# GENConv in a four-layer graph network: two float16 parts in four stored passes instead of three bf16 parts per tile, and other layer ends

## The reference

```python
def _genconv(x, src, dst, W1, W2, gamma, beta, t):
    msg = jax.nn.relu(x[src]) + EPS_MSG
    w = _segment_softmax(msg * t, dst, n)
    aggr = jax.ops.segment_sum(msg * w, dst, num_segments=n)
    h = x + aggr
    h = h @ W1                                  # 128 -> 256
    mu = h.mean(axis=0)
    var = h.var(axis=0)
    h = (h - mu) * jax.lax.rsqrt(var + EPS_BN) * gamma + beta
    h = jax.nn.relu(h)
    return h @ W2                               # 256 -> 128
for l in range(3):
    h = jax.nn.relu(_genconv(h, src, dst, W1[l], W2[l], gamma[l], beta[l], t[l]))
```

## Time and profile before

| | us |
|---|---|
| runs of the kernel before, median of 2 (least, greatest) | 2631.39 (2630.99, 2631.8) |
| the profiled execution, its own time | 2630.21 |
| its span, first to last instruction | 2628.5 |
| PE, PEld, DVE, ACT, POOL busy | 2110.8, 1458.5, 1622.6, 878.1, 1362.6 |
| `genconv`, first instruction to the next stage's first (1226.3 to 2006.4) | 780.1 |
| its three layers, first scatter to first scatter | 256.1 and 256.0; the last to its end 255.7 |
| mean granted TensorE clock over the span (share of 2.4 GHz) | 0.796 |

### The profile page before, as it was taken

One profiled execution on the slowest core, in us unless ns is written; L12 is line 12 of the kernel. 1 busy time (PEld: TensorE's weight loads), 2 busy tenths in 40 slices (PEclk: granted clock), 3 DMA queues, 4 the chain that ended last, 5 costly groups with the idle time before them and its releaser, 6 DMA issues. The chain is left out here.

```text
span 2628.5 us, 46839 instructions
## 1 busy us (share of the span) xinstructions
PE 2110.8 (80%) x9373; PEld 1458.5 (55%) x9374; DVE 1622.6 (62%) x5060; ACT 878.1 (33%) x1968; POOL 1362.6 (52%) x1338
## 2 busy tenths in 40 slices
PE   3588687887989999987999699979987566667766
PEld 1266555547888888874555355435545345545554
DVE  7999521125777777755257625752674677777775
ACT  1499411111212222212111311131113466666663
POOL 2300000003777777751777277637871677777771
PEclk9999788887555555557999799989997677777777
DMA  0000100002444444431111011101113222222221
GB/s 10 4 0 0 39 1 0 0 2 87 120 117 119 118 118 118 118 109 31 17 17 17 9 17 17 15 10 17 17 19 110 73 64 65 64 66 64 64 65 37
DMA packets 197087, 128.42 MB, mean 49 GB/s; under 512 B 138144, under 2 KB 179993, under 8 KB 195872
## 3 DMA queue, kind: packets, MB, share of 16 engines
q0 software_dynamic: 40256, 60.21, 10.2%
q1 hardware_dynamic: 151820, 59.71, 8.8%
q10 hardware_dynamic: 4822, 6.56, 0.8%
HBM read 106.83 MB, written 13.34 MB: 46 GB/s over the span
## 5 line engine op out<-in xcount | busy, mean ns | idle before, releaser
L1783 PE MATMUL ps<-adj,extra 125*128 (+2 forms) x3150 | 606.5, 354 | 35.0 <-DVE extra L1589 35.0
L1480 POOL DMA_INDIRECT edge_rows<-pay,small x425 | 511.7, 1204 | 129.2 <-issue 127.7
L1783 PEld LDWEIGHTS ps<-adj,extra 125*128 125x128 bf16 x3150 | 308.8, 98 | 332.1 <-issue 41.5
L1962 POOL DMA_INDIRECT adj<-h_rows,adj x416 | 396.2, 952 | 136.2 <-issue 65.5
L1157 POOL DMA_INDIRECT work<-p_rows,small x416 | 396.0, 952 | 126.8 <-issue 98.1
L2139 PE MATMUL ps<-adj 128*128 128x125 f32 x928 | 207.1, 360 | 164.2 <-DVE work L2040 159.8
L2139 PEld LDWEIGHTS ps<-adj 128*128 128x128 f32 x928 | 170.8, 254 | 258.5 <-issue 159.2
L1324 PE MATMUL ps<-work 128*128 x1024 | 300.3, 448 | 17.1 <-DVE work L1215 15.5
L1335 PE MATMUL ps<-small,work 128*128 128x64 f32 x1024 | 254.2, 403 | 36.2 <-issue 34.6
L1335 PEld LDWEIGHTS ps<-small,work 128*128 128x128 f32 x1024 | 241.9, 326 | 57.2 <-issue 55.3
L1324 PEld LDWEIGHTS ps<-work 128*128 128x128 f32 x1024 | 238.5, 322 | 26.5 <-issue 23.8
(11 more groups left out here) (347 smaller groups left out, 3015.2 us busy)
## 6 DMA issues: line engine op xcount, KB each, us to landing
work<-dst_all SPq DMA_DIRECT2D x256, 64.0 KB
work<-edge_attr SPq DMA_DIRECT2D x256, 64.0 KB
edge_rows<-pay,small POOLq DMA_INDIRECT x425, 2.7
work<-p_rows,small POOLq DMA_INDIRECT x416
adj<-h_rows,adj POOLq DMA_INDIRECT x416
adj<-adj SPq DMA_DIRECT2D x232, 24.0 KB
pay<-edge_pay SPq DMA_DIRECT2D x106, 46.9 KB
work<-x_kept SPq DMA_DIRECT2D x2, 1562.5 KB, 6.6
```

The source lines that it names most:

```text
L1480: eng.indirect_dma_start(edge_rows[:, :], bass.IndirectOffsetOnAxis(ap=place[:, k:k + 1], axis=0), pay[:, k * ROW:(k + 1) * ROW], None).th ...
L1783: ins = eng.matmul(ps[:, j, 0:cw], parts[k][:, i * D:(i + 1) * D], cols, start=first and i == 0, stop=last and i == 2, skip_group_check=True)
L1962: eng.indirect_dma_start(gathered[:, at:at + D], None, h_rows[:, :], bass.IndirectOffsetOnAxis(ap=row3_i[:, c, DST_C:DST_C + 1], axis=0)). ...
```

## The change

- **Parts.** Instead of three bf16 parts of e and of e*msg there are two float16 parts. The high part is rounded by adding and subtracting `GRID`, the low part is the rest times 2048 (`SPLIT`); the sums of the low part are divided by 2048 when they are read. Values are scaled to at most 32768 (`LARGE`).
- **Passes.** The parts are stored for all tiles, and PE runs four passes over A instead of two: high of e, low of e, low of e*msg, high of e*msg, 175 matmuls each, 700 a layer. Six tiles at a pass's end (four in the second pass) and six at the beginning of the last two are taken piece by piece, so that a PSUM bank is complete, or is needed, one after the other. DVE reads each bank behind each pass (four reads a layer).
- **Who makes them.** The exponent moves to ACT (three activations a tile: exponent, exp, low part), DVE has the weighting, the high part and the rest (three operations a tile). The ring `e` has six tiles.
- **Denominators.** Inverted in 7 pieces of 450 columns during the third pass.
- **Bands.** `BAND` 64 to 4 and `REACH` 70 to 11.
- **Layer end.** x is added with the sums; the second half's relu and the read-outs are shared between ACT and DVE in another way; all of h @ W2's first halves come before the second halves; the greatest values, the transposes and the messages follow piece by piece.
- **Order in the code.** The layers are written out one after the other instead of a loop. The scatters stay where they are: 136, 136, 153, behind the all-reduce and the clearing of each layer. DVE now waits for the clearing (`s_acc`) before the layer's first tile instead of in the middle. `GIN_TURNS` is 0.

```diff
-BAND = 64.0
-REACH = 70.0
+BAND = 4.0
+REACH = 11.0
+LARGE = 32768.0
+SPLIT = 2048.0
+GRID = 768.0
+RINGS, APART = 6, 4
+HEAD, TAIL = [0, 0, 6, 6], [6, 4, 6, 6]
+MARKS = [10, 11, 12, 13, 14, 15, 16]
+GIN_TURNS = 0
...
+    def high_of_exp(s):
+        return high_e_last if isinstance(s, int) and s == NT - 1 else high_e[:, column(s)]
+
+    def low_of_exp(s):
+        return low_e_last if isinstance(s, int) and s == NT - 1 else low_e[:, column(s)]
+
+    def low_of_sum(s):
+        return high_of_exp(s)
+
+    def high_of_sum(s):
+        return apart[:, column(s - FROM)] if isinstance(s, int) and s >= FROM else low_of_exp(s)
+
+    def part_of(p, s):
+        return (high_of_exp, low_of_exp, low_of_sum, high_of_sum)[p](s)
```

SP and POOL:

```diff
+            fill(TURNS - GIN_TURNS, 0, NC - TURNS * 2 * SC)
+            eng.wait_ge(s_x, AL * NP)
+            eng.wait_ge(s_sc[0], 16 * ((TURNS - GIN_TURNS) * SC + NC - TURNS * 2 * SC))
+            eng.wait_ge(s_sc[1], 16 * (TURNS - GIN_TURNS) * SC)
...
-            with eng.Fori(0, AL) as l:
+            for l in range(AL):
                 eng.wait_ge(s_spread, l + 1)
-                eng.nop(nofuse=True)
                 eng.partition_all_reduce(top, lim, D, bass.bass_isa.ReduceOp.max).then_inc(s_top, 1)
 
-                eng.wait_ge(s_copied, 1)
-                eng.wait_ge(s_saved, 16)
-                eng.wait_ge(s_fin, l + 1)
+                if l == 0:
+                    eng.wait_ge(s_copied, 1)
+                    eng.wait_ge(s_saved, 16)
+                    eng.wait_ge(s_max, NP)
+                    eng.wait_ge(s_tr, NGR)
+                else:
+                    eng.wait_ge(s_x, l * NP)
                 eng.memset(acc, 0.0).then_inc(s_acc, 1)
                 with eng.Fori(0, EACH) as i:
                     for b in SETS:
-                        scatter(l * EACH + i, b)
-            for q in range(AL * EACH, TURNS):
+                        scatter(i + l * EACH, b)
+            for q in range(AL * EACH, TURNS - GIN_TURNS):
                 for b in SETS:
                     scatter(q, b)
-            scatter(TURNS, 0, NC - TURNS * 2 * SC)
```

DVE, the band count and the tiles:

```diff
-                step(eng.tensor_tensor(spread, top[:, 0:1], top[:, 1:2], ALU.add))
-                step(eng.tensor_scalar(spread, spread, BAND - REACH, 1.0 / BAND, ALU.add, ALU.mult))
...
+                step(eng.scalar_tensor_tensor(spread, top[:, 0:1], BAND - REACH, top[:, 1:2], ALU.add, ALU.add))
+                step(eng.tensor_scalar(spread, spread, 1.0 / BAND, 0.0, ALU.mult, ALU.max))
+                eng.tensor_scalar(ranges[0:1, l * 2:l * 2 + 1], spread[0:1, :], float(1 << 19), 1.0,
+                                  ALU.min, ALU.add).then_inc(s_band, 1)
...
+                    def high(n):
+
+                        q, s = ORDER[n]
+                        eng.wait_ge(s_w, r * TILES + (n + 1))
+                        if n == 0:
+                            eng.wait_ge(s_sum, r * (4 * NP) + 1)
+                        if q == 1 and s < FROM:
+                            eng.wait_ge(s_used, r * FROM + (s + 1))
+                        eng.tensor_scalar(high_of_sum(s) if q else high_of_exp(s), e[n % RINGS], GRID, -GRID,
+                                          ALU.add, ALU.add).then_inc(s_hi, 1)
+
+                    def rest(n):
+
+                        q, s = ORDER[n]
+                        k = n % RINGS
+                        eng.wait_ge(s_hi, r * TILES + (n + 1))
+                        eng.tensor_tensor(e[k], e[k], high_of_sum(s) if q else high_of_exp(s),
+                                          ALU.subtract).then_inc(s_rest, 1)
...
+                    def produce(n, end):
+                        if n + 2 < end:
+                            weighted(n + 2)
+                        rest(n)
+                        if n + 1 < end:
+                            high(n + 1)
```

DVE, the reads between the passes and the denominators:

```diff
+                    def sum_of(p, j):
+                        eng.wait_ge(s_sum, r * (4 * NP) + (p * NP + j + 2))
+                        return ps[:, j, 0:PIECES[j][2]], den[:, PIECES[j][1]:PIECES[j][1] + PIECES[j][2]]
+
+                    def add_to_x(p, j, scale):
+
+                        y, w = sum_of(p, j)
+                        _, c0, cw = PIECES[j]
+                        eng.scalar_tensor_tensor(y, y, scale, w, ALU.mult, ALU.mult).then_inc(s_num, 1)
+                        eng.wait_ge(s_num, r * (2 * NP) + ((p - 2) * NP + j + 1))
+                        if l == 0 and p == 2 and j == 0:
+                            eng.wait_ge(s_copied, 1)
+                        eng.scalar_tensor_tensor(x[:, c0:c0 + cw], y, widest[:, 0:1], x[:, c0:c0 + cw],
+                                                 ALU.mult, ALU.add).then_inc(s_read, 1)
...
+                    eng.wait_ge(s_mask, r * NP + NP)
                     for j, c0, cw in PIECES:
-                        eng.wait_ge(s_sum, r * (2 * NP) + NP + j + 2)
-                        d, ac = den[:, c0:c0 + cw], acc[:, c0:c0 + cw]
-                        eng.tensor_tensor(d, ps[:, j, 0:cw], d, ALU.mult).then_inc(s_num, 1)
-                        eng.wait_ge(s_num, r * NP + j + 2)
...
+                    def accepted(j):
+                        w = den[:, PIECES[j][1]:PIECES[j][1] + PIECES[j][2]]
+                        eng.wait_ge(s_inv, r * NP + (j + 1))
+                        eng.scalar_tensor_tensor(w, w, float(np.exp(REACH) / LARGE), w, ALU.is_le,
+                                                 ALU.mult).then_inc(s_weight, 1)
+
+                    for j, c0, cw in PIECES:
+                        w = den[:, c0:c0 + cw]
+                        eng.reciprocal(w, w).then_inc(s_inv, 1)
+                        if j:
+                            accepted(j - 1)
+                    accepted(NP - 1)
+                    eng.wait_ge(s_weight, r * NP + NP)
+                    for j in range(NP):
+                        add_to_x(2, j, 1.0 / SPLIT)
+                    for j in range(NP):
+                        add_to_x(3, j, 1.0)
+                    eng.memset(later, 1e37).then_inc(s_more, 1)
+                    eng.tensor_scalar(shift_s, shift_s, -BAND, None, ALU.add).then_inc(s_shift, 1)
                 eng.wait_ge(s_w1, l * 32 + 32)
```

ACT, the tiles:

```diff
+                    def exponent(n):
+
+                        if n == 0:
+                            eng.wait_ge(s_lo, r * TILES + 1)
+                        if n >= RINGS:
+                            eng.wait_ge(s_lo, r * TILES + (n - RINGS + 2))
+                        eng.activation(e[n % RINGS], of_node(ORDER[n][1]), ACT.Relu, bias=shift_s[0:P, :],
+                                       scale=minus_t[0:P, l:l + 1]).then_inc(s_y, 1)
+
+                    def exponential(n):
+                        eng.wait_ge(s_y, r * TILES + (n + 1))
+                        eng.activation(e[n % RINGS], e[n % RINGS], ACT.Exp, scale=-1.0).then_inc(s_e, 1)
+
+                    def low(n):
+
+                        q, s = ORDER[n]
+                        eng.wait_ge(s_rest, r * TILES + (n + 1))
+                        if n == 0:
+                            eng.wait_ge(s_sum, r * (4 * NP) + 1)
+                        if n == NT:
+                            eng.wait_ge(s_sum, r * (4 * NP) + NP + 1)
+                        eng.activation(low_of_sum(s) if q else low_of_exp(s), e[n % RINGS], ACT.Copy,
+                                       scale=SPLIT).then_inc(s_lo, 1)
```

PE, the passes:

```diff
+                    def ready(p, s):
+
+                        at = s if p < 2 else s + (NT + APART)
+                        eng.wait_ge(*((s_hi, r * TILES + (at + 1)) if p in (0, 3) else (s_lo, r * TILES + (at + 2))))
+
+                    def product(p, s, j, last):
+                        _, c0, cw = PIECES[j]
+                        first = isinstance(s, int) and s == 0
+                        if first:
+                            eng.wait_ge(s_read, r * (4 * NP) + (p * NP + j + 1))
+                        if isinstance(s, int):
+                            cols = adj[:, s, c0:c0 + cw]
+                        else:
+                            cols = adj[:, bass.ds(s, 1), c0:c0 + cw].rearrange("p o c -> p (o c)")
+                        ins = eng.matmul(ps[:, j, 0:cw], part_of(p, s), cols, start=first, stop=last,
+                                         skip_group_check=True)
...
+                            ins.then_inc(s_sum, 1)
+                        return ins
+
+                    for p in range(4):
+                        by_piece = NT - TAIL[p]
+                        if HEAD[p]:
+                            ready(p, HEAD[p] - 1)
+                            for j in range(NP):
+                                for s in range(HEAD[p]):
+                                    product(p, s, j, False)
+
+                        def tile(s):
+                            ready(p, s)
+                            for j in range(NP):
+                                ins = product(p, s, j, False)
+                            if p == 1:
```

(44 more changed lines are left out.)

465 lines of the change are left out of this document (209 added, 256 removed).

## The result

The change takes **2517.54 us** (median of 2 runs, 2515.03 to 2520.05) against 2631.39: ratio 0.9567, 95% interval 0.9544 to 0.959. The profiled execution took 2520.05 us (span 2518.3); forecast were 2519, and 2507 to 2546 as the range.

What follows compares the result with a forecast made beforehand. PE bounds the kernel before; after the change POOL's scatters set genconv's layers (208.3 us instead of 256.1). Scatters and turnarounds end at 1885.9, the next stage starts at 1895.4 instead of 2006.4: 2630.2 - 111.0 = 2519 us, range 2507 to 2546.

Steps and rivals of the forecast that it cites:

- Products: PE's matmuls in a genconv layer: 700 instead of 1050 at 192.5 ns, 134.8 us, 67.4 less a layer.
- Parts ready in time: ACT (1.11 us a tile) and DVE (1.00) keep up with PE (1.35); 0 stalls, upper end 15 us a pass boundary.
- Layer ends: PE's time in a genconv layer outside the products: 26.9 to 53.9 us, against 53.9 before.
- POOL's path: A layer's 136 scatters (204.8 us) plus all-reduce and clearing: 208.3 us, longer than PE's 162 to 189.
- The stage's end: After genconv's last scatter, ending at 1885.9 us, x is copied back and the next stage begins at 1895.4.
- Clearing at 0: POOL's clearing, now of 16-bit words, could save 0 to 1.4 us a layer; counted as 0.
- Scatters under another load: POOL's time per scatter in genconv: today's mix kept; bounds 8 us less to 41 us more in sum.
- The rival of 1.30 us: Genconv's scatters stretch to 1.30 us each: 2560 us in all, 41 more; chance 0.07.
- rival 4: TensorE's clock falls within genconv's passes: 313 us a layer, 2801 us in all, slower than before; chance 0.03.
- Bands: One band in each genconv layer; rival of two in all three: about 2830 us, chance 0.02.
- PE's slack: PE's idle time in a genconv layer, waiting for POOL's all-reduce behind the scatters: 19 to 46 us.
- rival 2: PE's path longer than POOL's through stalls and layer ends: 2586 us at worst, middle 2545; chance 0.07.

Runs made afterwards that it cites:

- gin17_plain: Changed kernel with 136 scatters moved to the GIN stage, without most of the piece order: genconv stage 566.3 us against 529.9 with it on the same chip.
- gin17: Changed kernel with 136 scatters (17 turns) moved from the genconv layers to the earlier GIN stage: 2788.99 us, 0.9187 of the kernel before; stage 524.9 us.
- gin8: Changed kernel with 64 scatters (8 turns) moved from the genconv layers to the earlier GIN stage: stage 566.6 us, period 185.3 us.
- after_again: The changed kernel itself, unaltered, run again on another chip than the result's: stage 663.8 us, period 210.0 us.
- before_gin17: The kernel before the change with 136 scatters moved to the GIN stage: ratio 0.9981 to the kernel before, stage 771.8 us, period 256.2 us.

## Why the prediction was right, step by step

- **Products:** 134.8 us a layer predicted, 135.6 measured on the result's chip. In the same order of pieces, 137 to 144 on two others and 154 to 172 on the third show that the price of one matmul from the earlier trace rows is a price of an undisturbed loop; where POOL is the bound, the difference costs nothing.
- **Parts ready in time, 0 for stalls between passes:** right on the result's chip, where the windows above are as full as those of the earlier trace rows. `gin17_plain` shows what the order by pieces does for it: without it the third and fourth pass begin with waits, and a layer is 12.8 us longer.
- **Layer ends, 26.9 to 53.9 us:** `gin17` gives 33.0 and 33.4 (last product to next first product), in the lower half. PE's path is then 169 on the result's chip (208.3 between two first products, less 46.22 idle, plus the 6.69 that follow the all-reduce in `gin17`) and 174 to 176 bare on the two other chips; predicted were 162 to 189.
- **POOL's path 208.3 us:** measured 209.9 and 208.9 from first scatter to first scatter. The scatters' first layer took 205.5 us from first to last start instead of 203.6, in part for one of 2002 ns; the turnaround took 3.2 instead of 3.5. `gin8` gives 1.48 us for a scatter taken out, and the sum had 1.506.
- **The stage's end:** the last scatter ended at 1886.5 (1885.9 predicted), SP issued the copy at 1887.96, and the next stage began at 1895.50 (1895.4). That these agree to 0.6 us is partly luck: the first scatter came 1.7 us earlier than set (1236.94; the bound was 3), which offset the longer first period.
- **Clearing at 0:** 2.77 us for 16-bit words as for 32-bit ones, so the half that I had bounded did not come.
- **Scatters under another load:** the mean went from 1204 to 1208 ns. The rival of 1.30 us had nothing for it.
- **The clock:** 0.98 and 0.99 over each run of products, so rival 4 stayed away. The dissenting rule that I had weighed, of the Trainium skill, TensorE: Matmul & The Clock Gate (section A second HAM failure mode: psum-queue depth-cycling), that going through the PSUM banks in each iteration makes the clock swing, is not borne out by this line either: seven banks in turn at 0.98.
- **Bands:** 150 exps of L1787, so one band in each layer.
- **What the prediction did not see:** how thin the cover can be. I had put PE's slack at 19 to 46 us; on the result's chip it is about 40 us (209.4 - 169), but on the chip of `after_again` products of 169 us leave 210.0 - (169 + 33.3) = 8 us. The forecast would still hold there (stage 663.8), with little to spare.
- **Two side sums were off.** From the mean of 1204 ns before, all scatters at 1182 would give 9 us less, not 8; and halfway between 2519 and 2586, the bounds of rival 2, lies 2552, not 2545. Neither moves the forecast.

So the change was worth 80 to 82 us a layer on PE (256.1 to 174.2 to 176.1) and gave 47 (256.1 to 209.4), since POOL's scatters stood behind. The mechanism that was forecast is the one that the runs show. `gin17` brings in most of the rest.

## What to carry to other kernels

Before pricing a faster engine, measure the idle time of the next one in the same loop: 48 us of POOL's idle time a layer, not the 67 of matmul time removed, was the size of this gain. When a change ends on a new bound, move that bound's work to a stage where its engine is idle; here 136 scatters lengthened an earlier stage by no more than 1 us and gave 121 us. And an edit that shows no effect under one bound (the order of pieces) has to be tried again once the bound has moved.

## What the runs showed of the hardware that was not expected

- PE's queue stands still inside a hardware loop on some chips. Register operations (one for each matmul) took 46 ns in the median everywhere, single ones up to 722 ns on one chip and 657 to 707 on two others, against 89 at most in the profiled execution of the result; more time lies in stretches of 0.3 us and more in which loader and queue show nothing (29.7 us in one layer of `after_again`, 7.1 in one of `gin17`). A loop of 7 matmuls a tile ran at 0.68 and 0.52 of its pace in the two windows above. The kernel before, with 840 register operations for 3150 matmuls, had none above 51 ns on one of these chips (`before_gin17`), and its products took 202 us there too. Whether fewer register operations a matmul would help was not tried; that nearly all of the stretches are in the second pass speaks against their number alone.
- The same kernel before took 2631, 3038 and 3212 us on different chips, while its `genconv` stage took 771.7 us on the first and 771.8 on the second (the latter in `before_gin17`). Up to the degree row, stored at 592.0 us, these two are equal as well; from there to the save of x lie 635 and 848 us, in the stage with row gathers. What slows it is open.
- A memset of 128 x 3125 elements on POOL took 2.77 us in bf16 as in f32.
- In `gin17` the scatters took 1193 ns in the mean beside `gin` and 1215 in `genconv`.
